# A gated cross-attention and mixture-of-experts layer: another order of the work between attention and the expert tiles

## The reference

```
x = x + tanh(g_xattn) * (softmax(q k^T / 4) v @ Wo.T + bo)    # q from layernorm(x), k and v from ctx
z = layernorm(x)
shared = swiglu(z @ sw1 + sb1) @ sw2 + sb2
probs  = softmax(z @ gate_w + gate_b)                          # 8 experts
routed = sum over the two best e of probs[e] * (swiglu(z @ rw1[e] + rb1[e]) @ rw2[e] + rb2[e])
x = x + tanh(g_ffn) * (shared + routed)
```

## Time and profile before

| what | us |
|---|---|
| median of three runs | 701.77 (699.82 to 703.7) |
| the profiled execution | 702.51, of which the profile's span is 700.7 |
| first expert tile turned on TensorE, from the span's start | 568.38 |
| TensorE busy in the span | 636.0 |

### The profile page before, as it was taken

The page is one execution under the profiler, slowest core; times in us unless marked ns, Lnnn a source line. Parts: engine busy times, 40 slices in busy tenths (PEclk is TensorE's granted clock), DMA queues, the critical chain, the costliest instruction groups (busy, mean ns, idle before and its releaser), DMA issues.

```text
span 700.7 us, 12736 instructions
## 1 busy us (share of the span) xinstructions
PE 636.0 (91%) x3616; PEld 331.2 (47%) x3616; DVE 482.7 (69%) x805; ACT 424.1 (61%) x842; POOL 230.8 (33%) x241
## 2 busy tenths in 40 slices
PE   3997769699999999999999999999988989999990
PEld 3775542223333333333333333345466778888880
DVE  4877878658888888888888888847676853334430
ACT  4675344567777777777777777776733224444440
POOL 2443142214422442244000211220057714555552
PEclk9999997989999999999999999999989999999995
DMA  7999889754696779667843661224179565655545
GB/s 237 343 270 346 200 265 163 123 72 108 120 202 184 172 153 211 185 163 151 178 59 62 91 106 32 91 83 159 36 256 326 203 187 87 103 93 96 77 46 142
DMA packets 82979, 108.22 MB, mean 154 GB/s; under 512 B 16552, under 2 KB 64690, under 8 KB 81973
## 3 DMA queue, kind: packets, MB, share of 16 engines
q1 hardware_dynamic: 72200, 78.97, 48.6%
q0 software_dynamic: 10736, 28.71, 15.5%
HBM read 62.10 MB, written 47.35 MB: 156 GB/s over the span
## 4 chain that ended last, share of the span: by engine, by line
PE 71%; issue 14%; DVE 5%; POOL 4%; DMA 3%; ACT 1%; POOLq 1%; SPq 0%; DVEq 0%; ACTq 0%
PE psO L1510 17%; PE psS L1483 16%; PE psM L1465 13%; PE psH L1728 7%; PE psY L1754 3%; POOL parts L616 3%; PE psH L1684 2%; PE psX L1578 1%; PE psH L1725 1%; PE psX L1716 1%; PE psH L1739 1%; DMA acc<-ysb,ids 1%; PE psO L1553 1%; DMA wA_raw<-wqkv 1%; PE psM L1483 1%
## 5 line engine op out<-in xcount | busy, mean ns | idle before, releaser
L1116 DVE TENSOR_REDUCE mneg<-psM 128x1 f32<-128x1024 f32 x240 | 282.7, 1219 | 67.9 <-PE psM L1465 67.6
L850 ACT ACTIVATE pr<-psS 128x512 f32<-128x512 f32 x488 | 266.7, 595 | 102.1 <-PE psS L1483 102.1
L1483 PE MATMUL psS<-kq 99*128 99x512 bf16 x488 | 153.7, 388 | 7.6 <-DMA kq<-msb 7.0
L1510 PE MATMUL psO<-pr,vt 128*32 128x512 f32 x1024 | 137.2, 608 | 0.0
L1465 PE MATMUL psM<-kq 96*128 96x512 bf16 x480 | 127.9, 387 | 4.3 <-DVE mneg L1116 2.6
L1483 PEld LDWEIGHTS psS<-kq 99*128 99x128 bf16 x488 | 39.9, 97 | 155.8 <-ACT pr L850 130.5
L757 POOL DMA_INDIRECT acc<-ysb,ids x39 | 60.2, 1543 | 66.5 <-ACT ysb L973 32.0
L1465 PEld LDWEIGHTS psM<-kq 96*128 96x128 bf16 x480 | 46.5, 98 | 63.4 <-DVE mneg L1116 8.9
L602 POOL TENSOR_TENSOR msb<-mcp,none 16x128 bf16<-16x128 f32 x16 | 6.2, 389 | 208.7 <-ACT mcp L827 208.6
L1728 PE MATMUL psH<-wall,zgT 128*128 x234 | 68.2, 427 | 0.0
L1354 DVE TENSOR_TENSOR rg<-psH,rs 128x256 f32<-128x256 f32 x39 | 16.5, 424 | 66.4 <-ACT rs L961 66.4
(11 more groups left out here) (244 smaller groups left out, 818.3 us busy)
## 6 DMA issues: line engine op xcount, KB each, us to landing
kq<-k_parts SPq DMA_DIRECT2D x96, 128.0 KB, 5.7
w_parts<-wraw POOLq DMA_DIRECT2D x14, 768.0 KB, 4.3
wall<-w_parts SPq DMA_DIRECT2D x7, 1536.0 KB, 7.6
v_pad<-vst SPq DMA_DIRECT2D x16, 512.0 KB, 9.1
vt<-v_pad SPq DMA_DIRECT2D x16, 512.0 KB, 7.7
wraw<-wexp POOLq DMA_DIRECT2D x9, 768.0 KB, 7.1
k_parts<-parts SPq DMA_DIRECT2D x16, 384.0 KB, 7.2
kq<-q_parts SPq DMA_DIRECT2D x96, 64.0 KB, 5.5
```

Source lines behind the costliest of these rows:

```text
L850: nc.scalar.activation(pr[:, slot, j], score_bank(s, j), ACT.Exp, scale=SCALE).then_inc(e_done, 1)
L1116: V.tensor_reduce(mneg[:, parity, i:i + 1], psM[:, i % 2], X_AXIS, ALU.max, negate=True).then_inc(m_free, 1)
L1483: mm(score_bank(s, j), kst[:, slot, j, kt * P:(kt + 1) * P], qst[:, slot, j], start=True, stop=True).then_inc(s_full, 1)
L1510: last = mm(psO[j * VW:(j + 1) * VW, u % 2], vt[:, u, k, j * VW:(j + 1) * VW], pr[:, k % 4, j], start=(k == 0), stop=(k == KT - 1), skip_g ...
```

## The change

On TensorE and VectorE the last unit's output now comes ahead of `r_choose(1)`, `r_shift(2)` and `r_slots(1)`, which leave attention's stages; the output of batch 3 is turned into a part of `psH` where it was `psY`, and the wait for `d_ok` moves from `r_attn(3)` to `r_wo(3)`. The shared expert's `first(b, j)` can be made in two halves, and the first one starts ahead of `r_prefix(1)`. VectorE's list of the tail is in another order. GpSimd writes `fill` in attention (unit 10) and no longer clears `brow1` and `brow2`: SyncE copies rows 3 to 127 of them from `fill`, and TensorE waits for five transfers on `brow_ld` where it waited for three. The removed `brow_ok` is not shown.

```diff
@@ -539,7 +539,10 @@
                     sp.dma_start(zs[bass.ds(row, P)], fill).then_inc(fill_st, 16)
             store_base(0)
 
-            sp.wait_ge(brow_ok, 2)
+            sp.wait_ge(h_full, 6)
+            sp.wait_ge(sc_done, 16 * 2 * QT * (NB - 1))
+            for rows_of, n in ((brow1, 2 * D), (brow2, D)):
+                sp.dma_start(rows_of[3:P].bitcast(F32), fill[3:P, 0:n // 2].unsqueeze(1).to_broadcast([P - 3, NE, n // 2])).then_inc(brow_ld, 16)
             b1_rows = b1_parts.rearrange("s (e c) -> s e c", e=NE)
             sp.dma_start(brow1[0:3, 0:NR], b1_rows[:, 1:NE]).then_inc(brow_ld, 16)
             sp.dma_start(brow1[0:3, NR:NE], b1_rows[:, 0:1]).then_inc(brow_ld, 16)
@@ -564,6 +567,9 @@
             store_base(2)
             store_base(3)
             for i in range(4, TILES_R):
+                if i == ZG - 1:
+
+                    sp.wait_ge(brow_ld, 80)
                 load_tile(i)
 
             sp.wait_ge(added, 16 * (TILES_R + 1))
@@ -687,6 +693,17 @@
                 pool.wait_ge(wp_st, 32 * e)
                 nc.gpsimd.dma_start(wraw[:, 0], wexp[raw_of(e)]).then_inc(raw_ld[0], 16)
 
+            def blank_rows():
+
+                pool.wait_ge(wp_st, 32 * LATE)
+                nc.gpsimd.memset(fill, 0.0).then_inc(fill_c, 1)
+                pool.wait_ge(fill_c, 1)
+                nc.gpsimd.tensor_copy(fill[:, 264:272].bitcast(U32), spare[:, 0:1].to_broadcast([P, 8])).then_inc(fill_ok, 1)
+                nc.gpsimd.tensor_copy(spare_ids.bitcast(U32), spare[:, 1:1 + SPARES].unsqueeze(2).to_broadcast([P, SPARES, 8])).then_inc(fill_ok, 1)
+                pool.wait_ge(fill_ok, 2)
+                nc.gpsimd.dma_start(acc[NB * NQ:].rearrange("(k p) d -> p k d", p=P),
+                                    fill[:, 0:D].unsqueeze(1).to_broadcast([P, 1 + SPARES, D])).then_inc(added, 16)
+
             for n in range(UNITS - 1):
                 if n >= UNITS - NG:
                     bias_x(n - UNITS + NG)
@@ -701,6 +718,8 @@
                         raw_in(0)
                 elif n < 2 + LATE:
                     stage(n - 2)
+                elif n == 3 + LATE:
+                    blank_rows()
             bias_x(NB - 1)
 
             def scatter(b):
@@ -718,14 +737,6 @@
             scatter(0)
             scatter(1)
 
-            pool.wait_ge(wp_st, 32 * LATE)
-            nc.gpsimd.memset(fill, 0.0).then_inc(fill_c, 1)
-            pool.wait_ge(fill_c, 1)
-            nc.gpsimd.tensor_copy(fill[:, 264:272].bitcast(U32), spare[:, 0:1].to_broadcast([P, 8])).then_inc(fill_ok, 1)
-            nc.gpsimd.tensor_copy(spare_ids.bitcast(U32), spare[:, 1:1 + SPARES].unsqueeze(2).to_broadcast([P, SPARES, 8])).then_inc(fill_ok, 1)
-            pool.wait_ge(fill_ok, 2)
-            nc.gpsimd.dma_start(acc[NB * NQ:].rearrange("(k p) d -> p k d", p=P),
-                                fill[:, 0:D].unsqueeze(1).to_broadcast([P, 1 + SPARES, D])).then_inc(added, 16)
             nc.gpsimd.iota(row_i[:, 0:16], pattern=[[P, 16]], base=0, channel_multiplier=0).then_inc(io_c, 1)
             nc.gpsimd.iota(row_i[:, 16:16 + TAB], pattern=[[1, TAB]], base=0, channel_multiplier=0).then_inc(io_c, 1)
             nc.gpsimd.iota(row_i[:, 16 + TAB:64], pattern=[[REGION, NR]], base=0, channel_multiplier=0).then_inc(io_c, 1)
@@ -736,10 +747,6 @@
             scatter(2)
             scatter(3)
 
-            pool.wait_ge(h_full, 6)
-            pool.wait_ge(sc_done, 16 * 2 * QT * (NB - 1))
-            nc.gpsimd.memset(brow1[:].rearrange("p e c -> p (e c)").bitcast(F32), 0.0).then_inc(brow_ok, 1)
-            nc.gpsimd.memset(brow2[:].rearrange("p e c -> p (e c)").bitcast(F32), 0.0).then_inc(brow_ok, 1)
 
             pool.wait_ge(base_st, 16 * NB)
             pool.wait_ge(tab_ok, 3)
@@ -874,7 +881,7 @@
             def r_attn(b):
                 act.wait_ge(at_full, b + 1)
                 for k in range(DT):
-                    nc.scalar.activation(aT[:, k], (psX if b < 3 else psY)[:, k], ACT.Identity,
+                    nc.scalar.activation(aT[:, k], (psX if b < 3 else psH[:, 1])[:, k], ACT.Identity,
                                          bias=bq_s[:, 2, k:k + 1]).then_inc(at_ok, 1)
 
             def r_high(b):
@@ -896,7 +903,7 @@
 
             beside_attention = {0: ((r_attn, 0),), 2: ((r_attn, 1),), 4: ((r_attn, 2),), 6: ((r_high, 0),), 7: ((r_logits, 0),),
                                 8: ((r_high, 1),), 9: ((r_exp, 0), (r_logits, 1)), 10: ((r_high, 2),),
-                                11: ((r_exp, 1), (r_logits, 2))}
+                                11: ((r_exp, 1),), 12: ((r_logits, 2),)}
 
             with act.Fori(0, NB - 1) as b:
                 for u in range(NG):
@@ -921,22 +928,22 @@
                 act.wait_ge(g_ok, 2 * b + j + 1)
                 nc.scalar.copy(g_parts(b)[0][:, j], g[:, j]).then_inc(gh_ok, 1)
 
+            r_attn(3)
             r_exp(2)
             nc.scalar.activation(warm[:], tg_in[:, 1:2], ACT.Silu)
-            r_attn(3)
 
             silu(0, 0)
+            silu(0, 1)
             gated_high(0, 0)
-            silu(0, 1)
+            r_high(3)
             silu(1, 0)
-            r_high(3)
             gated_high(0, 1)
+            r_logits(3)
             silu(1, 1)
             gated_high(1, 0)
-            r_logits(3)
             r_exp(3)
+            silu(2, 0)
             gated_high(1, 1)
-            silu(2, 0)
             silu(2, 1)
             gated_high(2, 0)
             gated_high(2, 1)
@@ -1283,7 +1290,7 @@
 
             beside_attention = {1: ((r_sum, 0), (r_scale, 0)), 3: ((r_sum, 1), (r_scale, 1)), 5: ((r_sum, 2),), 6: ((r_low, 0), (r_scale, 2)),
                                 8: ((r_shift, 0), (r_low, 1)), 9: ((r_choose, 0),), 10: ((r_shift, 1), (r_low, 2)),
-                                11: ((r_slots, 0), (r_choose, 1)), 12: ((r_shift, 2), (r_slots, 1))}
+                                11: ((r_slots, 0),)}
 
             with dve.Fori(0, NB - 1) as b:
                 for u in range(NG):
@@ -1311,32 +1318,35 @@
                 V.scalar_tensor_tensor(out=rows, in0=psB(b)[:].rearrange("p a (t d) -> p (a t) d", d=D), scalar=tg[:, 1:2],
                                        in1=rows, op0=ALU.mult, op1=ALU.add).then_inc(y_taken, 1)
 
+            r_choose(1)
+            r_shift(2)
+            r_slots(1)
             r_choose(2)
+            r_sum(3)
+            gate(0, 0)
             r_slots(2)
-            gate(0, 0)
+            r_scale(3)
             gated_low(0, 0)
-            r_sum(3)
-            r_scale(3)
             gate(0, 1)
+            r_low(3)
             gate(1, 0)
-            r_low(3)
             gated_low(0, 1)
-            gated_low(1, 0)
             gate(1, 1)
             r_shift(3)
+            gated_low(1, 0)
             r_choose(3)
+            gated_low(1, 1)
             r_slots(3)
             r_counts()
-            gated_low(1, 1)
             gate(2, 0)
+            base(0)
             gate(2, 1)
-            r_table()
-            r_table_rest()
-            base(0)
             gated_low(2, 0)
             gated_low(2, 1)
+            r_table()
+            base(1)
+            r_table_rest()
             gate(3, 0)
-            base(1)
             gate(3, 1)
             gated_low(3, 0)
             gated_low(3, 1)
@@ -1560,12 +1570,11 @@
                 else:
 
                     pe.wait_ge(o_taken, UNITS + 1)
-                    pe.wait_ge(d_ok, b)
                 if b:
 
                     pe.wait_ge(wo_taken, b)
                     pe.wait_ge(at_ok, 2 * b)
-                src, dst = (a_in, psX) if b < NB - 1 else (a_last, psY)
+                src, dst = (a_in, psX) if b < NB - 1 else (a_last, psH[:, 1])
                 for k in range(DT):
                     for t in range(QT):
                         last = tr(dst[:, k, t * P:(t + 1) * P], src[:, t, k * P:(k + 1) * P], idn[:])
@@ -1573,6 +1582,9 @@
 
             def r_wo(b):
                 pe.wait_ge(at_ok, 2 * b + 2)
+                if b == NB - 1:
+
+                    pe.wait_ge(d_ok, b)
                 for t in range(QT):
                     for k in range(DT):
                         last = mm((psX if b < 3 else psY)[:, t // 2, (t % 2) * D:(t % 2 + 1) * D], aT[:, k, t * P:(t + 1) * P], wo_s[:, k],
@@ -1635,8 +1647,7 @@
 
             beside_attention = {0: ((r_attn, 0),), 1: ((r_wo, 0),), 2: ((r_attn, 1),), 3: ((r_wo, 1),), 4: ((r_attn, 2),),
                                 5: ((r_wo, 2),), 6: ((r_turn, 0),), 7: ((r_logits, 0),), 8: ((r_lturn, 0), (r_turn, 1)),
-                                9: ((r_logits, 1),), 10: ((r_lturn, 1), (r_turn, 2)), 11: ((r_prefix, 0), (r_logits, 2)),
-                                12: ((r_lturn, 2), (r_prefix, 1))}
+                                9: ((r_logits, 1),), 10: ((r_lturn, 1), (r_turn, 2)), 12: ((r_prefix, 0),)}
 
             with pe.Fori(0, NB - 1) as b:
                 for u in range(NG):
@@ -1672,36 +1683,42 @@
```

(36 more changed lines are left out.)

2 lines of the change are left out of this document (1 added, 1 removed).

## The result

The changed kernel takes 710.13 us (median of four, 705.44 to 714.17), the kernel before 702.01 beside it (699.82 to 703.7). The ratio is 1.009, 95% interval 1.005 to 1.013: 8 us slower. The forecast was 715, so the sign and the range held and the size was 5 us too large: 13 us were forecast, and 8 came.

The account below looks back on a forecast made before the run. Expert tiles keep TensorE busy, so only the first tile's turn can move, bound by the shared expert and by SyncE's DMA chain. 702.5 + 11.5 (later turn) + 1.5 (lower clock) = 715.5, 714.8 beside the median, said as 715; range 697 to 728.

Parts of the forecast that it names:

- batch 3 normalised: VectorE's normalising of batch 3 in the tail: ends at 528.9 in place of 532.9, 4.0 us earlier.
- counts: VectorE's counts behind batch 3: at 544.5 against 548.49, 4.0 us earlier.
- shared expert ends: TensorE's last shared expert matmuls ahead of tile 0: end at 562.5, 5.5 us earlier than 568.02.
- first fill issued: SyncE's first SBUF to SBUF fill, behind eight stores and one base store: issued at about 551.
- first tile turned: TensorE's start on the expert tiles: at 579.9 against 568.38, 11.5 us later.
- The first chain: TensorE with VectorE up to the shared expert's end: reordered work gains 4.0 us at the normalising, 5.5 at that end.
- the clock: TensorE's half clock from 516 to 518: perhaps spared, put at nothing, with 1.5 us either way in the range.
- The number of engines: DMA engines sharing each fill of 125 rows: five, 25 rows each, as rows are dealt whole and equally.
- a packet costs the same at either size: Fill packets on a DMA engine: 47 ns each, whether of 1 KB or 512 bytes.
- the term of 21.2 us for the fills: Both fills on each of five DMA engines: 450 packets at 47 ns, ending at 572.7 from 551.5.
- The rival of wide fills: Fills spread over 15 or 16 engines, done near 560; first tile 3.5 to 5 us earlier, 697.5 us; chance 0.22.
- the wide fills that gain less than their bound: Fills spread wide but the new TensorE and VectorE order gains nothing: 701 to 703 us; chance 0.02.

Follow-up runs that it names:

- old order with fills: Kernel before with GpSimd's two clears replaced by SyncE's two fills of 125 rows: 1.018 on the first chip, again 1.018 (717.2 us) on the fourth.
- 124 rows: Changed kernel with each fill cut into rows 4 to 127 and row 3 alone: 734.4 us, 1.026 of the kernel before.
- kernel with 512-byte pieces: Changed kernel with both fills in pieces of 512 bytes, 3375 packets instead of 2250, same bytes: 712.02 us, 1.013 of the kernel before.
- wide fills: Changed kernel with each fill cut into 112 and 13 rows: 1.011, 0.995 and 0.999 of the kernel before on the first, third and fourth chip.
- new order with clears: Changed kernel with GpSimd's two clears behind its last scatter in place of SyncE's fills: 1.007 on the first chip, 0.999 (703.75 us) on the second.

## Why the prediction was right in direction and wrong in size

The steps, in the forecast's own order, each from the split of maxima:

| step | forecast | measured after | old order with fills, full clock |
|---|---|---|---|
| unit's output written | +45.0 | +44.8 | +49.5 |
| batch 3 normalised | +62.7 | +62.6 | +64.3 |
| counts | +78.3 | +77.1 | +78.3 |
| list of tiles done | +88.8 to 90.8 | +88.8 | +86.1 |
| last scatter issued | +87.8 | +87.4 | +90.9 |
| shared expert ends | +96.3 | +95.05 | +97.6 |
| first fill issued | +84.8 | +83.2 | +87.8 |
| from there to the first tile's turn | 28.9 | 24.6 | 23.3 |
| first tile turned | +113.7 | +107.8 | +111.05 |
| tile 0 to the end, over before | +1.5 | +1.8 | +1.6 |

*The first chain: the times right, their cause in part.* The sum over VectorE's row of work met the new kernel's times within 1.3 us. But the forecast takes the whole difference to before, 4.0 us at the normalising and the counts, for the order's own work, and the clock at nothing. The last column says otherwise: against an old order at full clock the new one is 1.7 us ahead at the normalising, 1.1 at the counts and 2.5 at the shared expert's end; the rest of 4.1, 5.2 and 6.7 is time that TensorE loses at half clock before. In before VectorE stands 2.35 us for TensorE ahead of `r_slots(2)`; at full clock it doesn't. So the clock, a term that the forecast put at nothing, goes with the larger part of this gain. Its times came out even so, because they were added up from VectorE's work alone, and after has no stretch below 1.00 ahead of the wait. By the medians of the fourth chip the new order is worth 4 to 4.7 us to the kernel as it ran there, the spared clock included. `fill` in attention cost nothing: three of GpSimd's splits stand 23.52 and 23.53 us apart after (342.95, 366.47, 390.00) as before (371.01, 394.54).

*The number of engines: right.* Five was read off the strips of three rows, and 125 and 124 rows gave 0.33 to 0.38 and 0.26 to 0.30 of the DMA engines. By the rule of the Trainium skill (DMA: Bandwidth & Descriptors, Why a DMA increments its semaphore by 16 and not by 1) these are five and four, and the traces agree, with 17.5 to 19 GB/s an engine for 512-byte pieces in both.

*The step that failed: "a packet costs the same at either size", 47 ns,* and with it the term of 21.2 us for the fills. Of the 5.9 us by which the first tile came earlier than forecast, 4.3 lie here and 1.6 in the earlier issue of the fills. Measured on these engines, a packet of 1 KB takes 43 ns and one of 512 bytes 27, so the fills are 225 x (43 + 27) ns = 15.8 us of each of five engines, not 21.2; with the scatters the stretch ended at about 564 (SyncE's next issue, 563.55), 18.6 us after its start at about 545.4, in place of 24.2. Of the 5.4 us between 21.2 and 15.8, 4.5 are the 512-byte pieces; the price for 1 KB was nearly right. The small loads, the base store and tile 0 behind it took 5.5, not 4.2. The kernel with 512-byte pieces only tells the two prices apart: it took 1.6 us more, where the price by packets makes it 10.6 and the price by bytes 2.5. The earlier trace rows was the wrong row for a price: its 323 packets are said to take 117.1% of 16 engines, more than there are, so the time put down to a packet there can't be the time that it holds an engine.

*The earlier issue:* the counts came 1.2 us earlier than forecast and the eight stores followed at once.

*The sum.* 5.7 (107.8 less 102.16) and 1.8 are 7.5 us, beside 8.1 between the medians. The forecast's terms are 11.5 and 1.5. Its chances don't quite add up as stated: the wide fills that gain less than their bound (0.02) belong to "same", which makes 0.10 and 0.70 where it has 0.08 and 0.72.

*The rival of wide fills, 697.5,* was too optimistic. Where no idle pieces disturb, the wide fills came out even with before (0.999, fourth chip), as the new order with clears did (0.999, second chip), and each for its own reason: tile 0 late and at half clock behind 4.2 us of idle, which gives back 2.6 of 2.8 us, and VectorE held by GpSimd. Neither was among the forecast's terms: the rival has no term for the clock, and of the clears it counted only GpSimd's own time.

*Open.* On the first and third chip before took 715 and 716 us, and every variant had idle pieces. They go with the chip (or the hour) and not with the kernel: four of these kernels ran without them on the second or fourth chip. What they are wasn't settled; full DMA queues aren't it. The ratios from those two chips carry them as well, and that may be why the wide fills have 1.011 and 0.995 there. Open too is why TensorE's clock falls in two of three executions of the old order and not in the third.

## What to carry to other kernels

Before moving a clear from an engine to a DMA, count how many engines its rows can be dealt to: 125 rows went to five, and 13 us were lost to save 3 us of GpSimd. Price a packet by its bytes on one engine, from a stretch in which only that transfer runs. Before calling a gain the order's, compare the granted clock of both profiles stretch by stretch: 4 us of 6.7 were clock here. When the order of an engine's list changes, look at what the shared neighbour does at that moment: the same two clears cost nothing beside one piece of VectorE's work and 3.6 us beside another, and letting the clears wait 0.55 us took that away.
